# VectorE's work per tile of the attend stage, split into 22 single steps in an interleaved order

## What is computed

```python
z = 1.0 / (einsum('blhd,bhd->blh', q_phi, k_sum) + 1e-06)
out = einsum('blhd,bhde,blh->blhe', q_phi, kv, z).reshape(...) @ Wo + bo
x = _layernorm(x + out, ln1_g, ln1_b)          # first norm (a)
ff = relu(x @ W1 + b1) @ W2 + b2
x = _layernorm(x + ff, ln2_g, ln2_b)           # second norm (b)
...                                            # the graph part and the old x are added
weights = _layernorm(x) @ wr + br              # third norm (c), then the router's weight
```

## Time and profile before

| | |
|---|---|
| median of 3 runs | 2607.99 us (2604.91 to 2608.49) |
| span of the profiled execution | 2735.8 us, mean granted TensorE clock 0.874 |
| the profiled execution's own time | not recorded; its span is 127.8 us above the median |
| attend stage in the profile | first matmul at 2055.94, next stage's first work at 2504.06 |
| PE, DVE, ACT, POOL busy over the span | 82%, 53%, 30%, 59% |

### The profile page before, as it was taken

How to read it: one execution, slowest core, us unless ns; L and a number is a source line. 1 busy time by engine, 2 the same in 40 slices (tenths; PEclk the granted TensorE clock), 3 DMA queues, 4 the chain that set the end, 5 groups by cost and what they waited for, 6 DMA issues and landing times. The chain is left out here.

```text
span 2735.8 us, 47046 instructions
## 1 busy us (share of the span) xinstructions
PE 2240.2 (82%) x12461; PEld 1829.5 (67%) x12462; DVE 1457.9 (53%) x4032; ACT 826.7 (30%) x2317; POOL 1616.4 (59%) x2089
## 2 busy tenths in 40 slices
PE   7876767767666766655889999989998999996898
PEld 5644555555554544444869999967767888885798
DVE  9754433434444454435842223259987777777211
ACT  2511221221111111111623333335553333332333
POOL 5676666666666666764036555447857666661232
PEclk9987787878877886676589999999999999997999
DMA  4233332322333333333323334323221111111121
GB/s 159 98 99 87 88 92 86 90 86 86 91 90 87 91 91 92 92 90 85 118 77 106 106 123 138 104 78 101 88 68 55 44 46 42 44 46 62 30 37 29
DMA packets 139022, 227.27 MB, mean 83 GB/s; under 512 B 26923, under 2 KB 99456, under 8 KB 138946
## 3 DMA queue, kind: packets, MB, share of 16 engines
q0 software_dynamic: 56240, 142.70, 18.8%
q1 hardware_dynamic: 81186, 82.10, 9.0%
q10 hardware_dynamic: 1520, 1.58, 0.2%
HBM read 174.97 MB, written 51.30 MB: 83 GB/s over the span
## 5 line engine op out<-in xcount | busy, mean ns | idle before, releaser
L945 POOL DMA_INDIRECT all_XN<-h_table,l_srcI x782 | 780.3, 998 | 367.3 <-issue 219.1
L1152 PE MATMUL gcn_acc<-all_XN,gcn_hot 128*128 128x256 f32 x796 | 257.6, 475 | 110.9 <-DVE all_X L1037 54.4
L1152 PE MATMUL gcn_acc<-all_XN 128*128 128x256 f32 x768 | 248.1, 478 | 110.9 <-DVE all_X L1037 59.5
L1152 PEld LDWEIGHTS gcn_acc<-all_XN,gcn_hot 128*128 128x128 f32 x796 | 179.1, 236 | 171.6 <-DVE all_X L1037 76.6
L1152 PEld LDWEIGHTS gcn_acc<-all_XN 128*128 128x128 f32 x768 | 175.2, 239 | 164.6 <-DVE all_X L1037 69.5
L879 ACT COPY gcn_seen_sb<-gcn_seen 128x392 f32<-128x392 f32 x98 | 47.6, 485 | 576.2 <-remote 454.8
L1848 ACT ACTIVATE moe_hidden<-moe_hid_ps,moe_b 128x128 f32<-128x128 f32 x420 | 131.5, 364 | 281.5 <-PE moe_hid_ps L1929 250.0
L1929 PEld LDWEIGHTS moe_hid_ps<-moe_xst,held_held 128*128 128x128 f32 x1680 | 204.2, 193 | 12.0 <-issue 7.4
L1037 DVE SCALAR_TENSOR_TENSOR all_X<-gcn_acc,all_XN,all_X 128x256 f32 x392 | 170.6, 475 | 74.7 <-remote 59.2
L1929 PE MATMUL moe_hid_ps<-moe_xst,held_held 128*128 128x128 f32 x1680 | 207.5, 277 | 1.9 <-DVE moe_xst L1869 1.9
L1045 DVE COPY_PREDICATED gcn_last_seen<-gcn_seen_sb,gcn_seen 128x392 f32<-128x392 int32 x98 | 57.7, 589 | 277.6 <-ACT gcn_seen_sb L879 190.1
(11 more groups left out here) (433 smaller groups left out, 4596.7 us busy)
## 6 DMA issues: line engine op xcount, KB each, us to landing
held_held<-in_e_w SPq DMA_DIRECT2D x32, 512.0 KB
slots_out<-moe_y SPq DMA_DIRECT2D x105, 128.0 KB
all_XN<-h_table,l_srcI POOLq DMA_INDIRECT x782
all_X<-in_x SPq DMA_DIRECT2D x7, 896.0 KB, 11.2
rows_table<-all_XN SPq DMA_DIRECT2D x7, 896.0 KB, 4.2
z_table<-held_held SPq DMA_DIRECT2D x49, 128.0 KB
x_table<-all_XN SPq DMA_DIRECT2D x49, 128.0 KB, 1.7
out<-all_X SPq DMA_DIRECT2D x49, 128.0 KB, 1.7
```

Of the source, the lines that this page charges most:

```text
L945: nc.gpsimd.indirect_dma_start(msg[b][:, c, :], None, self.h_table, bass.IndirectOffsetOnAxis(self.srcI[:, GE * g + c:GE * g + c + 1], 0)) ...
L1152: last = nc.tensor.matmul(acc[b % NA][:, :], hot[b % NH][:, c, :], msg[b][:, c, :], start=(c == 0), stop=(c == n - 1))
```

## The change

The eight steps of VectorE become 22 steps of mostly one instruction each (`digits` runs in one turn only, and `last_output` for one tile only). The instructions that do the work are the same ones with the same operands. Three things differ. The list is ordered so that two neighbours nearly always belong to different tiles or norms. In the first two norms the pass that subtracts the mean and multiplies by the gain (`scale_a`, `scale_b`) now stands ahead of the reciprocal and waits for the moments alone. And the last part of the third norm (`inverse_c`, `rows_c`, `weigh`, with `last_output`) has lag 5 in place of 4: it runs one turn later. On ScalarE the roots of a and c change places. The wait for the router's weight after every tile goes; the next `weigh` waits for the one before, and the last tile's for all.

```diff
-staggered(act, [(1, copy_ot), (3, relu(0)), (4, root(norm_b)), (3, relu(1)), (2, copy_xpt), (4, root(norm_c)), (1, root(norm_a))])
+staggered(act, [(1, copy_ot), (3, relu(0)), (4, root(norm_b)), (3, relu(1)), (2, copy_xpt), (1, root(norm_a)), (4, root(norm_c))])
...
-def attention(t, p, h):
+def head_sums(t, p, h):
     after(dve, qk_ready, t + 1)
     nc.vector.tensor_reduce(total[:, :], qk[p][:, :].rearrange("p (h e) -> p h e", e=HEAD), AX_X, ALU.add).then_inc(total_ready, 1)
+
+def denominators(t, p, h):
     after(dve, total_ready, t + 1)
...
-    norm_stats(nc, dve, norm_b, y2[:, :], t)
-def norm_2(t, p, h):
+    norm_sums(nc, dve, norm_b, y2[:, :], t)
+def moments_b(t, p, h):
+    norm_moments(nc, dve, norm_b, t)
+def scale_b(t, p, h):
-    norm_scale(nc, dve, norm_b, t)
+    after(dve, norm_b.var_ready, t + 1)
     nc.vector.scalar_tensor_tensor(scaled2[:, :], y2[:, :], norm_b.mv[:, 0:1], vecs["ln2_g"][:, :], ALU.subtract, ALU.mult).then_inc(scaled2_ready, 1)
+def inverse_b(t, p, h):
+    norm_inverse(nc, dve, norm_b, t)
+def rows_b(t, p, h):
     after(dve, scaled2_ready, t + 1)
+    after(dve, norm_b.rstd_ready, t + 1)
     after(dve, x_based, t + 1)
...
-staggered(dve, [(4, fed_forward), (0, attention), (0, digits), (4, norm_2), (1, attended), (4, norm_3), (1, norm_1), (4, last_output)])
+staggered(dve, [(4, fed_forward), (5, inverse_c), (0, head_sums), (0, digits), (4, sums_b), (5, rows_c), (0, denominators), (4, moments_b),
+                (5, weigh), (0, inverses), (4, scale_b), (0, divide), (4, inverse_b), (1, attended), (4, rows_b), (1, sums_a),
+                (4, sums_c), (1, moments_a), (4, moments_c), (1, scale_a), (1, inverse_a), (1, rows_a), (5, last_output)])
```

More of the change, by code:

```diff
@@ L2445, in attended, with sums_a, moments_a, scale_a @@
                         nc.vector.tensor_tensor(y[:, :], wo_ps[:, :], XN[:, ds(t * KVW, D)], ALU.add).then_inc(y_ready, 1)
+                    def sums_a(t, p, h):
                         after(dve, y_ready, t + 1)
-                        norm_stats(nc, dve, norm_a, y[:, :], t)
-                    def norm_1(t, p, h):
-                        norm_scale(nc, dve, norm_a, t)
+                        norm_sums(nc, dve, norm_a, y[:, :], t)
+                    def moments_a(t, p, h):
+                        norm_moments(nc, dve, norm_a, t)
+                    def scale_a(t, p, h):
+                        after(dve, norm_a.var_ready, t + 1)
                         nc.vector.scalar_tensor_tensor(scaled[:, :], y[:, :], norm_a.mv[:, 0:1], vecs["ln1_g"][:, :], ALU.subtract, ALU.mult).then_inc(scaled_ready, 1)
+                    def inverse_a(t, p, h):
+                        norm_inverse(nc, dve, norm_a, t)
+                    def rows_a(t, p, h):
                         after(dve, scaled_ready, t + 1)
+                        after(dve, norm_a.rstd_ready, t + 1)
                         after(dve, xp_turned, t - 1)
@@ L2460, in fed_forward, with sums_b @@
                         nc.vector.tensor_tensor(y2[:, :], f_ps[:, :], xpb[p][:, :], ALU.add).then_inc(y2_ready, 1)
+                    def sums_b(t, p, h):
                         after(dve, y2_ready, t + 1)
-                        norm_stats(nc, dve, norm_b, y2[:, :], t)
-                    def norm_2(t, p, h):
-                        x = X[:, ds(t * D, D)]
+                        norm_sums(nc, dve, norm_b, y2[:, :], t)
+                    def moments_b(t, p, h):
+                        norm_moments(nc, dve, norm_b, t)
@@ L2470, in norm_2, with sums_c @@
+                    def rows_b(t, p, h):
+                        x = X[:, ds(t * D, D)]
                         after(dve, scaled2_ready, t + 1)
+                        after(dve, norm_b.rstd_ready, t + 1)
                         after(dve, x_based, t + 1)
                         nc.vector.scalar_tensor_tensor(x, scaled2[:, :], norm_b.rs[:, 0:1], x, ALU.mult, ALU.add).then_inc(x3_ready, 1)
+                    def sums_c(t, p, h):
                         after(dve, x3_ready, t + 1)
-                        norm_stats(nc, dve, norm_c, x, t)
@@ L2476, in norm_3, with moments_c @@
[L2476 to L2480, removed]
+                        norm_sums(nc, dve, norm_c, X[:, ds(t * D, D)], t)
+                    def moments_c(t, p, h):
+                        norm_moments(nc, dve, norm_c, t)
@@ L2481, in norm_3, with inverse_c, rows_c, weigh @@
+                    def inverse_c(t, p, h):
+                        norm_inverse(nc, dve, norm_c, t)
+                    def rows_c(t, p, h):
+                        after(dve, norm_c.rstd_ready, t + 1)
+                        nc.vector.tensor_scalar(XN[:, ds(t * KVW, D)], X[:, ds(t * D, D)], norm_c.mv[:, 0:1], norm_c.rs[:, 0:1],
+                                                ALU.subtract, ALU.mult).then_inc(x4_ready, 1)
+                    def weigh(t, p, h):
                         after(dve, x4_ready, t + 1)
-                        nc.vector.scalar_tensor_tensor(products[:, :], xn, 1.0, vecs["wr"][:, :], ALU.mult, ALU.mult,
+                        after(dve, weight_ready, t)
+                        nc.vector.scalar_tensor_tensor(products[:, :], XN[:, ds(t * KVW, D)], 1.0, vecs["wr"][:, :], ALU.mult, ALU.mult,
@@ L2483, in norm_3 @@
                                                        accum_out=self.route[:, ds(t, 1)]).then_inc(weight_ready, 1)
-                        after(dve, weight_ready, t + 1)
+                        if isinstance(t, int) and t == T - 1:
+                            dve.wait_ge(weight_ready, T)
                     def last_output(t, p, h):
```

2 lines of the change are left out of this document (added).

## The result

| | before | after |
|---|---|---|
| median of 4 runs each | 2606.98 us (2604.91 to 2608.49) | 2583.02 us (2582.41 to 2585.51) |
| span of the profiled execution | 2735.8 us | 2583.8 us (its own time 2585.51) |
| mean granted TensorE clock over the span | 0.874 | 0.906 |
| attend stage, first `turn_o` to the next stage's first work | 448.12 us | 423.98 us |

The ratio is 0.9908, with a 95% interval from 0.9896 to 0.9919: 24.0 us less. The prediction was 2584, in a range from 2578 to 2600, with 0.85 on faster.

What follows compares the result with a forecast made beforehand. VectorE's 8.90 us turn, with gaps between dependent neighbours, was taken to hold TensorE above 8.33. Savings of 23.3, 1.3 and 0.5 less 0.4 lost gave 24.7 us, so 2584 us from 2607.99, range 2578 to 2600.

Steps and rivals of the forecast that it cites:

- 39 turns: Attend stage, tiles 8 to 47: TensorE's turns fall from 8.93 to 8.33 us, 23.3 us saved.
- turn from tile 47 to 48: End of the attend loop: this turn falls from 9.61 to 8.33 us, 1.3 us saved.
- first turns, to tile 3: Attend's start: the scaling pass runs during ScalarE's root, in two turns TensorE waits for; about 0.5 us saved (0 to 1).
- drain, after tile 48: Attend's end: three instructions of tile 47 stand behind tile 48's `fed_forward`; 0.4 us lost (0 to 1).
- One for one or in proportion: Converting the profiled gain of 24.7 us to the median: one for one 2583.3 us, in proportion 2584.5; 2584 was taken.
- rival that timed runs are less bound by VectorE than the profiled one: Attend loop: VectorE's gaps hold the profile's 4.9% excess, so the gain is 12 us, time 2596; chance 12%.
- The price of a border: VectorE's loop: independent neighbours start 0.08 us early; 20 such borders bring its turn from 7.44 to 5.84 us.
- flush that the Trainium skill describes: VectorE: every instruction is followed by a flush the next cannot pass, so order gains nothing, 2608 us; 2%, within another's 6%.
- if the 0.12 comes with every wait on a register, it stays: Rival, VectorE's loop: the gap belongs to the loop, not the neighbour; turn about 9 us, no change, 2608; chance 6%.
- VectorE's own turn: VectorE in the attend loop needs 6.5 us a turn (6.1 to 7.7), under TensorE's 8.33.
- meetings with GpSimd: Rival: denser VectorE passes meet GpSimd's six additions, 0.59 us each, turn 10.0 us, time 2651; chance 5%.
- The anchors: Attend turn: VectorE waits for `feed_out` before `fed_forward` and `project` before `attended`; nothing on TensorE's path is late.

## Why the prediction was right

**What bounded the kernel.** Right. VectorE's turn of 8.90 lay above TensorE's 8.33, and TensorE followed it; with VectorE below, every turn is 8.33, and with eight reductions added the old chain is back. The wait view alone would have shown the loss too small (0.2 us a turn for `feed_out`); reading it from the turn starts was what gave the size.

**The sum, term by term.**

| term | predicted | in the profiles |
|---|---|---|
| 39 turns | 23.3 saved | 348.15 - 324.93 = 23.22 saved |
| turn from tile 47 to 48 | 1.3 saved | 9.61 - 8.33 = 1.28 saved |
| first turns, to tile 3 | 0.5 saved (0 to 1) | 19.72 - 19.63 = 0.09 saved |
| drain, after tile 48 | 0.4 lost (0 to 1) | 29.43 - 28.98 = 0.45 lost |
| stage | 24.7 | 24.14 |

The medians give 23.96. The first turns are the term that was mis-sized. The eleven small instructions of `digits`, which run in one turn only, now stand ahead of tile 1's denominators, and the second `turn_o` comes 5.79 us after the first instead of 3.89. They take 1.4 of those 1.9 us (from 1930.14 to 1931.52); the denominators and `divide` behind them took 0.34 and 0.87 in place of 0.23 and 0.42. The next two turns make that up again and no more. I had not priced that move.

**One for one or in proportion.** I chose between 2583.3 and 2584.5 without a row that placed the profile's excess. The gather's line above places it outside the stage, so one for one was the right conversion. The measured 2583.02 agrees, but can't decide it: the interval of the ratio is a gain of 21 to 27 us, and both conversions lie in it. The rival that timed runs are less bound by VectorE than the profiled one falls by the gain itself, 24 us where it gave 12.

**The price of a border.** The early starts of 0.07 to 0.09 came, at nearly all borders. The flush that the Trainium skill describes (page "VectorE: DVE Perf Modes", section "The DRAIN you can't avoid") would have left the order worth nothing. The two orders of the same instructions, 9.51 and 8.33 us a turn, do not agree with that as a rule for every neighbour, and do agree with the section's remark on instructions that aren't held. What I had wrong is the cause of the 0.15. I gave all of it to the dependence, which by itself costs 0.03, and held the loop's part to be a rival, "if the 0.12 comes with every wait on a register, it stays". It does come with the loop, but not with every wait on a register: the eleven gaps that I counted are those with an instruction of the sequencer between, and the earlier trace rows already had two dependent passes without one, at 0.04. It doesn't stay either: behind an independent neighbour that instruction runs while the neighbour still works. The rival was half right in its mechanism and wrong in its conclusion. The forecast's own step, that an independent neighbour removes the whole gap, held, for a reason that I hadn't seen.

**VectorE's own turn.** 6.5 (6.1 to 7.7) was predicted, 6.7 worked out from the eight reductions. The nearness is partly luck. I took the meetings with GpSimd for little; they cost four passes 1.05 us a turn, and the sign by which I said I'd be wrong, such passes growing towards 1 us, is in the profile (means of 0.78 and 0.77 for `scale_b` and `scale_a`, 0.94 for `divide`). What kept the forecast is that this rival decides only from 2.4 us a turn on. The 1.07 of the earlier trace rows, by which I priced a meeting with an addition, met something else for most of its time. GpSimd's timeline of before beside that pass (2096.79 to 2097.86) has the gather's issue first and an addition only at the end:

```profile
2096.34 1.15 POOL L2358 DMA_INDIRECT held_held<-z_table,att_row  x1 [0.27 <-POOL att_row L2356]
2097.51 0.93 POOL L2365 TENSOR_TENSOR all_X<-all_X,held_held 128x256 f32<-128x256 f32 x1
```

The Trainium skill's page "SBUF — State Buffer", section "SBUF: two separate sides", has the shared ports as a lock for the whole instruction. That two-input passes lose beside GpSimd's work and recover without it agrees; at 2107.47 and 2108.13 the passes took 0.74 and 0.94, which is 0.27 and 0.47 over the 476 ns that the second pass of norm b takes on average, and less than the 0.68 to 0.93 of one addition.

**The anchors.** As drawn: VectorE waits for `project` ahead of `attended` and for `feed_out` ahead of `fed_forward`, GpSimd for the third norm's row (51.4 / 40 = 1.3 us a turn, so it has room), and nothing of TensorE waits. `rows_a` shows its wait of 0.27 for the reciprocal in 20 of 40 turns.

**Open.** Which of the loop's three kinds of sequencer instruction would cost how much alone no run settles, nor whether the order needs the pass ahead of the reciprocal and ScalarE's exchange.

## What to carry to other kernels

Look at the distance between the same instruction of two turns on the engine that should be the limit, and at each engine's gaps whose releaser is its own instruction just ahead: 98% busy on TensorE and 79% on VectorE hid 24 us. Then look which dependent neighbours have no such gap, and what the loop puts between the others. Such gaps go by putting another tile's instruction between, or, where an instruction of the sequencer stands in them, by writing the loop out; once the engine is below the limit, doing both or adding lags brought nothing more here. Level with the limit is not below it: see where the engine stands in the other's turn at the first tile and at the last. Before a gain is scaled from a profile to the medians, find the stage in which the profile's excess lies.

## What had not been expected of the hardware

An instruction of VectorE's sequencer that carries the wait, between two working instructions of which one needs the other, makes the second start 0.15 us behind the first in place of 0.03 to 0.04; a wait on a register's value that stands on the working instruction itself does not. Behind an independent neighbour nothing of it is seen. Writing 53 turns out gained as much here as the whole new order (0.9917 and 0.9908), without its room.

A denser VectorE meets GpSimd more: four passes over two rows went from between 0.48 and 0.58 to between 0.61 and 0.95 us, and two of them back to 0.45 and 0.48 once nothing of GpSimd's ran beside them. In the written-out kernel even an addition on 8 columns took 501 ns on average in place of 227.
